# Attention stage: two VectorE steps moved, the output projection in two parts, idle products left out

## The reference, cut to what matters

```
q, k, v = x @ Wq + bq, x @ Wk + bk, x @ Wv + bv        # x: layer-normed h, (32, 164, 192), 12 heads of 16
scores  = einsum('bhqd,bhkd->bhqk', q, k) * SCALE
scores  = where(abs(i - j) <= 64, scores, -inf)
attn    = softmax(scores, axis=-1)
out     = einsum('bhqk,bhkd->bhqd', attn, v)
h       = h + (out @ Wo + bo)
```

## Time and profile before

| | us |
|---|---|
| three runs | 2431.01, 2413.91, 2407.28 |
| median | 2413.91 |
| profiled execution, its own time | 2431.3 |
| its span, first to last instruction | 2429.6 |
| mean granted PE clock | 0.97 |
| PE, DVE, ACT, POOL busy | 2313.0, 1877.6, 1397.1, 250.7 |
| attention stage | about 330 to 880 of the span |

### The profile page before, as it was taken

How to read it: one execution, slowest core, us unless ns; L and a number is a source line. 1 busy time by engine, 2 the same in 40 slices (tenths; PEclk the granted TensorE clock), 3 DMA queues, 4 the chain that set the end, 5 groups by cost and what they waited for, 6 DMA issues and landing times.

```text
span 2429.6 us, 48876 instructions
## 1 busy us (share of the span) xinstructions
PE 2313.0 (95%) x20040; PEld 2162.5 (89%) x20040; DVE 1877.6 (77%) x2364; ACT 1397.1 (58%) x1391; POOL 250.7 (10%) x133
## 2 busy tenths in 40 slices
PE   6599989999999889999999999989999999999999
PEld 5266778888887779999999999989999999999999
DVE  7599756666665568676676766679999999999995
ACT  5398304444443373443534435488888888888881
POOL 7522100000000012121121211000000000000000
PEclk9799999999997789999999999999999999999999
DMA  6565241111111100000000001120000000000000
GB/s 203 160 155 151 69 157 34 47 47 46 47 47 34 39 22 21 26 19 21 21 19 26 19 15 34 64 84 23 23 23 23 23 23 23 23 23 23 23 18 10
DMA packets 99326, 115.82 MB, mean 48 GB/s; under 512 B 15271, under 2 KB 90551, under 8 KB 98487
## 3 DMA queue, kind: packets, MB, share of 16 engines
q1 hardware_dynamic: 79087, 89.38, 12.2%
q10 hardware_dynamic: 16520, 14.34, 2.0%
q0 software_dynamic: 3616, 10.54, 1.7%
HBM read 83.36 MB, written 30.86 MB: 47 GB/s over the span
## 4 chain that ended last, share of the span: by engine, by line
PE 63%; issue 0%; DVE 0%
PE spline_acc L1917 27%; PE spline_acc L1890 10%; PE spline_acc L1889 9%; PE spline_acc L1891 9%; PE spline_acc L1911 5%; PE spline_acc L1913 2%; PE spline_xT L764 0%; DVE spline_f L1666 0%; DVE spline_weights_low L1649 0%; DVE spline_x L1736 0%; DVE spline_x L1739 0%
## 5 line engine op out<-in xcount | busy, mean ns | idle before, releaser
L1917 PE MATMUL spline_acc<-spline_weights,spline_f 128*128 128x192 f32 x3936 | 670.7, 327 | 0.0
L1917 PEld LDWEIGHTS spline_acc<-spline_weights,spline_f 128*128 128x128 f32 x3936 | 635.9, 190 | 0.0
L1890 PE MATMUL spline_acc<-spline_f,spline_weights_high 128*128 128x328 f32 x1536 | 482.9, 314 | 0.0
L1889 PE MATMUL spline_acc<-spline_f,spline_weights_high 128*128 128x328 f32 x1536 | 480.2, 313 | 2.5 <-DVE spline_weights_low L1649 2.5
L1891 PE MATMUL spline_acc<-spline_f,spline_weights_low 128*128 128x328 f32 x1536 | 476.8, 310 | 0.0
L1889 PEld LDWEIGHTS spline_acc<-spline_f,spline_weights_high 128*128 128x128 f32 x1536 | 290.4, 189 | 2.8 <-DVE spline_weights_low L1649 2.8
L1890 PEld LDWEIGHTS spline_acc<-spline_f,spline_weights_high 128*128 128x128 f32 x1536 | 289.4, 188 | 0.0
L1891 PEld LDWEIGHTS spline_acc<-spline_f,spline_weights_low 128*128 128x128 f32 x1536 | 289.1, 188 | 0.0
L1911 PE MATMUL spline_acc<-spline_weights_split,spline_f_high 128*128 128x384 f32 x656 | 218.2, 389 | 8.2 <-issue 8.2
L1666 DVE SCALAR_TENSOR_TENSOR spline_f<-spline_front 128x984 fp32r<-128x984 f32 x128 | 145.5, 1177 | 100.3 <-PE spline_acc L1891 94.9
L1021 DVE TENSOR_REDUCE attend_max<-scores_by_query 82x6 f32<-82x876 f32 x128 | 136.3, 1065 | 47.9 <-PE scores_by_query L1352 47.2
(11 more groups left out here) (229 smaller groups left out, 4282.4 us busy)
## 6 DMA issues: line engine op xcount, KB each, us to landing
spline_front<-pos_scr SPq DMA_DIRECT2D x32, 540.0 KB, 4.4
hid_scr<-spline_hid SPq DMA_DIRECT2D x64, 164.0 KB, 1.8
spline_xn<-hid_scr SPq DMA_DIRECT2D x41, 256.0 KB, 3.1
attend_spread<-rec_scr SPq DMA_DIRECT2D x128, 61.5 KB, 2.2
pix_scr<-spline_front SPq DMA_DIRECT2D x32, 225.0 KB, 3.1
spline_weights_raw<-w SPq DMA_DIRECT2D x1, 6144.0 KB, 21.4
spline_weights<-w SPq DMA_DIRECT2D x4, 1536.0 KB, 6.1
spline_x<-h_scr SPq DMA_DIRECT2D x41, 96.0 KB, 1.9
```

The costliest lines, as they stand in the source:

```text
L1889: nc.tensor.matmul(z, high, x_high, start=start, stop=False)
L1890: nc.tensor.matmul(z, high, x_low, start=False, stop=False)
L1917: last = nc.tensor.matmul(z, f_rest[i][:, cols], w2[:, i, r, :], start=False, stop=stop)
```

## The change

On DVE, `norm_in` (and the spline stage's `norm_in`, in the last but one pair) goes from before `maximum` 0 to behind it. `residual` goes from behind `maximum` 0 to behind `maximum` 1. `invert(t - 1, 1)` goes from before the two `low_x` to behind them. On PE, `project_out` is issued in two halves, one for each 82 rows: the first behind `queries_scores` 0, the second behind `queries_scores` 1. Only the first half claims the bank and waits for `weigh`, only the second signals the bank as filled. The four idle products ahead of `queries_scores` 1 of each second block are gone; those of the first pair go from 13 to 6. In the last pair's second block (`finish`) and behind the loop `project_out` stays whole.

```diff
@@ DVE, pair
                     if i == 1:
                         invert(t, 0)
-                    if i == 1 and more2:
-                        norm_in(tt + 1, u)
-                    if i == 1 and spline:
-                        front.norm_in(nc, dve, 0)
                     for q in range(4):
                         if q == 3 and i == 1 and more2:
                             norm_out(tt + 1, u, use(t, X[1]))
                         if i == 0 or more:
                             maximum(nxt, q)
-                        if q == 0 and not first:
-                            residual(tt - 1 if u == 0 else tt, v, i, use(t, (Y_LAST if last else Y)[i]))
+                        if q == 0 and i == 1 and more2:
+                            norm_in(tt + 1, u)
+                        if q == 0 and i == 1 and spline:
+                            front.norm_in(nc, dve, 0)
                         if q == 1:
-                            if i == 0 and not first:
-                                invert(t - 1, 1)
+                            if not first:
+                                residual(tt - 1 if u == 0 else tt, v, i, use(t, (Y_LAST if last else Y)[i]))
                             if i == 0 and more:
                                 for j in range(2):
                                     low_x(t + 1, j, use(t, X[j]))
+                            if i == 0 and not first:
+                                invert(t - 1, 1)
@@ PE
-            def project_out(a, i, at):
-                bank = claim(at)
-                pe.wait_ge(weighed, a + 1)
-                for n in range(2):
+            def project_out(a, i, at, halves=(0, 1)):
+                bank = at[0]
+                if halves[0] == 0:
+                    claim(at)
+                    pe.wait_ge(weighed, a + 1)
+                for n in halves:
...
-                last.then_inc(filled[bank], 1)
+                if halves[-1] == 1:
+                    last.then_inc(filled[bank], 1)
@@ PE, pair
-                        if q == 1 and i == 1 and more:
-                            keep_going(13 if first else 4, xb[:, claim(use(t, V[0])), 0:HG * P])
+                        if q == 1 and i == 1 and first:
+                            keep_going(6, xb[:, claim(use(t, V[0])), 0:HG * P])
                         if nxt:
                             queries_scores(a + 1, w, 1 - i, q)
-                        if q == 0 and not first:
-                            project_out(a - 2, i, use(t, Y[i]))
+                        if q < 2 and not first:
+                            project_out(a - 2, i, use(t, Y[i]), (q,))
```

## The result

The changed kernel takes 2426.93 us (median of 22 runs, 2401.9 to 2442.36) against 2414.12 us of the kernel before (22 runs, 2395.26 to 2450.23). The ratio is 1.0053, 95% interval 1.0032 to 1.0075: slower by half a per cent, where 2403 us was forecast, in a range of 2394 to 2420.

A forecast was written before the change was run, and what follows sets the result against it. PE bounds the kernel, held up in turn by its own work and the single score buffer. 2409.2 (without late sums) - 4.2 (14 pairs) - 0.7 (first pair) = 2404.3, or 2402.4 from the lowest run; taken 2403, range 2394 to 2420.

The forecast's parts named there:

- The transposition's wait: First block: the second `turn_x` waits about 0.5 us on PE for `residual`, now behind `maximum` 1.
- quarter 2: Second block: PE's third quarter of scores starts at 626.75 in place of 627.56, 0.81 us gained.
- The idle products: Second block: 0.7 us of idle products only covered PE's wait for `maximum`; removing them costs nothing.
- a new PE wait of about 1.0 us: First pair's second block: PE waits ahead of quarter 2, which still gains 0.7 us; counted as -0.7 us.
- no such wait on PE is over 0.7 us: Moving `invert` shrinks late-sum waits; three clock falls go, removing 22 us from an execution like the profiled one.
- late sums: Row sums loaded late for `invert`, still late after the change; rival that they still strike: 2413 us, chance 0.07.
- the second block's `weigh`: It needs the later `invert`'s result through two DMAs; some 3 to 4 us of cover were left.
- The clock falls in ordinary pairs: Rival: without idle products and with new first-block PE waits, most pairs have a fall; 2466 us, chance 0.08.
- its variant of a few falls: A fall behind the first pair's new wait alone, or in one or two pairs: 2408 to 2412 us, chance 0.10.
- the 1.33 us at 582.46: A PE wait after late row sums without a clock fall, used as evidence against falls in ordinary pairs.
- my 4.5 us: Cost of one clock fall, first block's invert to the second's: 16.53 us with it, 11.99 us without.
- the store ahead of ACT's exponentials: Second block: exponentials come about 1.2 us later against quarter 2, hidden from `mix` with about 1 us of cover.

The follow-up runs named there:

- e2: Kernel before with only the idle products removed (four in each second block, 13 to 6 in the first pair): 2428.1 us, ratio 1.0042.
- e3: Changed kernel with the idle products put back (four in each second block, 13 in the first pair): 2413.6 us, ratio 0.9998.
- e13: Changed kernel with four idle products ahead of the two transpositions of a first block and nowhere else: 2410.5 us, ratio 0.9983.
- e9: Kernel before with only the first pair's idle products cut from 13 to 6, the four of every second block kept: 2415.1 us, ratio 1.0015.
- e5: Changed kernel with idle products set only in PE's waits, ahead of the first block's transpositions and the key projections: 2415.0 us, ratio 0.9986.
- e7: Changed kernel with the first block's projection whole again behind quarter 0 and its residual behind `maximum` 0: 2407.9 us, ratio 0.9973.
- e8: e7 with four idle products in the waits ahead of the key projections: 2413.8 us, ratio 0.9978.
- e12: Kernel before with `norm_in` moved behind `maximum` 0 and idle products out (13 to 6 in the first pair, four to none elsewhere): 2463.4 us, ratio 1.0206.
- e14: e11 with `norm_in` moved and the four idle products ahead of quarter 1 out: 2422.4 us, ratio 0.9974.
- e11: e6 with more idle products in the waits at the attention stage's ends: 2385.8 us, ratio 0.9891.
- e4: Kernel before with only the inverse of the previous pair moved behind the two `low_x`: 2407.2 us, ratio 0.9970.
- e1: Kernel before run again against itself, no edit: 2413.4 us, ratio 1.0005.
- e6: e4 with four more idle products in the waits ahead of the key projections: 2400.6 us, ratio 0.9925.

## Why the prediction was wrong

**The pair.** The steps were right and their sizes off. The transposition's wait was forecast at 0.5 us and measured 0.66; the query projections were to be 0.53 us late and are 0.66; quarter 2 was to gain 0.81 and gains 0.75. The first half of the projection costs 1.23 us (622.46 to 623.69), not 1.05; the second takes 1.04 ahead of the transpositions (624.48 to 625.52). The prediction had seen the 0.23 us more that the whole takes ahead of row-tiled products and had left them out of the half. Net 0.11 us a pair in place of 0.3. This moved the sum by 3 us and not across the sign.

**The idle products.** The step that failed reads "The 0.7 us of idle products was cover for the `maximum`, and goes with it at no price." Its price is clock. With only the products out (e2) the mean clock goes from 0.976 to 0.970 and the time up by 0.4%. Put back into the changed kernel (e3), or put into the one new wait (e13), they bring back 13 and 17 us, though in e3 they lengthen every pair by 0.6 us. The first pair has a share in it that the prediction put at nothing: it forecast "a new PE wait of about 1.0 us" there and measured 0.96, and such a wait has a fall behind it in five of eight profiles (see e9).

**The falls.** The second failed step reads "So no such wait on PE is over 0.7 us, and the three clock falls behind them go." I took a fall as the consequence of a long wait. In its old place the wait for late sums did go (outside the first and last pair PE's longest wait for a `maximum` is 0.59 us, and it no longer waits for `low_x`). But a longer one came in another place, 1.60 us for `weigh` at 437 us, with one of the trace's two falls ahead of the last pair behind it. It is in a first block; the prediction looked at the second block's `weigh` alone, and gave it 3 to 4 us of cover. PE waits for `weigh` in ordinary pairs in all six profiles that have the projection in halves and the residual behind `maximum` 1, in both blocks or in the second alone (the changed kernel, e3, e5, e7, e8, e13), and in none of the other ten. And falls come behind shorter waits too, in some pairs and not in others. I count the waits of PE at full clock between 400 and 800 us, in all sixteen profiles, and those with a fall in them or within 3 us behind: 12 of 13 at 1.5 us and more, 3 of 14 at 1.1 to 1.5, 11 of 26 at 0.85 to 1.1 (ten of the eleven in e12 and e14), none of 3 at 0.7 to 0.85, 2 of 38 at 0.6 to 0.7, both in e2. That a fall isn't settled by the wait alone shows in a place that the change leaves alone, the first pair's first block. The changed kernel's row is

```profile
374.05 0.66 PE L1329 MATMUL scores_by_query<-attend_k,attend_q 32*82 32x146 f32 x12 [1.53 <-DVE attend_max L1021]
```

Fourteen of the profiles have this wait, 1.52 to 1.56 us each time (e11 and e14 fill it). Within 3 us behind it a fall starts in four of them (the changed kernel, e2, e4, e5) and in ten none. The same wait is followed by a fall in one execution and by none in another.

**The rival that came nearest.** "The clock falls in ordinary pairs" has the mechanism, missing idle products and new waits, and its variant of a few falls (2408 to 2412 us, chance 0.10) is nearest in time. I dismissed it because the clock hadn't fallen behind the 1.33 us at 582.46. One survival of a draw says nothing about 28 more draws in each execution. With the pair's true size my sum is 2409.2 - 1.5 - 0.7 = 2407 us; the median is 20 us over it. The price of a fall was too low as well: my 4.5 us end at the second block's invert and are of the shortest of the three falls, and e12's falls of 10 to 14 us lengthen their pairs by 4 to 6 us. The changed kernel's profiled execution is at 2428 us, close to its median. From its first `low_x` to its last it takes 456.1 us, against 439.9 in e1's profile, where no fall lies between. That is 16 us, and 17.7 with the 1.5 us that the pairs save: two falls, of 17 and 24 us, with the waits ahead of them. So the 20 us are two or three falls, not one or two at 4.5 us.

**A reading.** The prediction put the dips of the clock line at 729 to 850 us. The line dips in the slice from 850 to 911 us too, the stage's end, which e11 then shortened, and in the second slice, ahead of the stage. No sum rests on this.

**Parts that held.** The late sums did land late in the new place too (ten waits of DVE for them, the longest 1.3 us), and the store ahead of ACT's exponentials cost PE nothing: no `mix` waits in an ordinary pair. One cover was thinner than said, that of the inverses for `weigh`, as told above. Whether the later store of `leave` or the later residual has a part in their coming late was not tried.

**Left open.** That the missing products and the uncovered wait cost clock is shown by runs (e2, e3, e13). Which of the changed kernel's waits the extra falls stand behind is not: its one trace shows none behind the 0.66 us wait that e13 fills, and no run takes away the wait for `weigh` alone. Open too is why e3, with the 0.66 us wait and four products elsewhere in the pair, has as good a clock as e13, and why e8's filled waits don't help. Missing products and uncovered waits both count, but not by their sum alone: PE's idle time in 29.2 us of an undisturbed stretch is 1.5 us before, 1.7 in the changed kernel and in e3, 2.1 in e2 and in e12, 1.1 in e13, 0.4 in e5, 0.6 in e6. e3 breaks that order, and e12, with e2's idle time in one longer wait, has much the lower clock.

## What to carry to other kernels

An idle product that lies in a wait costs no time (the pairs of e5, e6 and e13 stay as they were), and taking it out can cost more than the wait it covered; before removing one, ask what wait of PE it leaves bare, and count how many times per execution. A wait that a reordering moves to PE should be weighed by what may follow it, not only by its length: filling 0.66 us in each of 14 pairs gave back 17 us and made no path shorter (e13). Joining two short waits into one longer one can be worse than both (e12). And look for waits that the reordering opens elsewhere, as here ahead of `weigh`. When the runs of a kernel spread by 2%, plot time against granted clock before reading one trace: here that separates work (1 us) from clock (10 us) at once.

## What the runs showed of the hardware

At one and the same wait of 1.5 us the clock falls in some executions and not in others (four of fourteen, above). Of the falls between 350 and 810 us in all profiles, the shortest lasts 3 us (e7, at 423) and the longest 24 us (the changed kernel, 438 to 462). The Trainium skill, page "TensorE: Matmul & The Clock Gate", section "What's actually happening", has activity as what releases the low clock. The runs agree, with products whose result nobody reads: filling three waits at the ends of one stage took the mean clock from 0.981 to 0.986 and the ratio to before from 0.9925 to 0.9891 (e6 to e11).
